# Four buffers instead of two for the second expert weights in an eight-core mixture-of-experts layer

## What is computed

```python
xn = layernorm(x)
att = (xn @ w_v.T + b_v) @ w_out.T + b_out          # softmax rows sum to 1
logits = xn @ router_w.T;  top2, idx = top_k(logits, 2);  w = softmax(top2)
h1 = gelu(xn @ w1[e].T + b1[e])                     # for each of 8 experts, 1024 -> 4096
y_e = h1 @ w2[e].T + b2[e]                          # 4096 -> 1024
out = x + att + sum over the two chosen e of w_e * y_e
```

## Time and profile before

| what | value |
|---|---|
| runs of the kernel before | 4571.72, 4616.52, 4870.86 us; median 4616.52 us |
| the profiled execution | 4570.31 us |
| its span on its slowest core (core 1) | 4568.8 us |
| TensorE matmul busy | 3863.4 us, 85% of the span |
| VectorE, ScalarE, GpSimd busy | 8%, 14%, 13% |
| weights moved by GpSimd's queue | 279.21 MB, 41.7% of the 16 DMA engines' time |

### The profile page before, as it was taken

How to read it: one execution, slowest core, us unless ns; L and a number is a source line. 1 busy time by engine, 2 the same in 40 slices (tenths; PEclk the granted TensorE clock), 3 DMA queues, 4 the chain that set the end, 5 groups by cost and what they waited for, 6 DMA issues and landing times.

```text
span 4568.8 us, 41331 instructions; the slowest of 8 cores (4540.7 to 4568.8 us)
## 1 busy us (share of the span) xinstructions
PE 3863.4 (85%) x17200; PEld 1662.0 (36%) x17200; DVE 372.7 (8%) x626; ACT 626.7 (14%) x610; POOL 575.3 (13%) x817
## 2 busy tenths in 40 slices
PE   2466889898989889898988989898988989898984
PEld 1222334343434334343433334343433434343431
DVE  4322010000000000100001010000000010000001
ACT  0122002030201112020201103020111202020200
POOL 1010111111111111111111011111111111111110
PEclk9687999999999999999999999999999999999997
DMA  4343344444444444444446244444444444453444
GB/s 76 51 60 50 43 64 70 64 70 60 74 60 73 63 66 68 60 72 60 75 60 142 45 62 72 60 76 56 72 64 67 67 62 72 60 81 53 72 61 101
DMA packets 251605, 307.02 MB, mean 67 GB/s; under 512 B 47591, under 2 KB 178663, under 8 KB 251424
## 3 DMA queue, kind: packets, MB, share of 16 engines
q0 software_dynamic: 244512, 279.21, 41.7%
q1 hardware_dynamic: 6912, 25.17, 1.7%
HBM read 574.89 MB, written 8.39 MB: 128 GB/s over the span
## 4 chain that ended last, share of the span: by engine, by line
PE 63%; DMA 25%; issue 5%; DVE 5%; ACT 1%; DVEq 0%; POOLq 0%; POOL 0%; SPq 0%; ACTq 0%
PE P L337 38%; PE P L416 22%; DMA wvw<-w2r 21%; DVE scr L430 3%; DMA wvw<-w1r 2%; DMA wvw<-wvf 1%; PE P L368 1%; PE P L187 1%; DMA x_rot<-x 1%; PE P L246 1%; ACT vg L349 1%; DVE xnF L252 0%; DMA b1c_sb<-b1c 0%; DVE scr L238 0%; DVEq L46 0%
## 5 line engine op out<-in xcount | busy, mean ns | idle before, releaser
L416 PE MATMUL P<-wvw,vg 128*128 128x512 bf16 x8192 | 1892.5, 385 | 394.5 <-DMA wvw<-w2r 335.1
L337 PE MATMUL P<-xnF,wvw 128*128 128x512 bf16 x8192 | 1787.1, 381 | 19.9 <-DMA wvw<-w1r 8.7
L416 PEld LDWEIGHTS P<-wvw,vg 128*128 128x128 bf16 x8192 | 778.7, 99 | 1505.9 <-issue 681.5
L337 PEld LDWEIGHTS P<-xnF,wvw 128*128 128x128 bf16 x8192 | 800.7, 98 | 1004.7 <-issue 57.9
L349 ACT ACTIVATE vg<-P,b1c_sb 128x1024 bf16<-128x1024 f32 x512 | 570.5, 1114 | 3224.7 <-PE P L337 3224.6
L393 POOL DMA_DIRECT2D wvw<-w2r x512 | 359.7, 703 | 2070.8 <-PE P L416 2001.8
L430 DVE SCALAR_TENSOR_TENSOR scr<-P,wmap_sb,scr 128x512 f32<-128x512 f32 x256 | 192.1, 750 | 3666.0 <-PE P L416 3642.0
L320 POOL DMA_DIRECT2D wvw<-w1r x256 | 180.0, 704 | 1585.3 <-PE P L337 1585.3
L187 PE MATMUL P<-xnF,wvw 128*128 128x512 bf16 x256 | 82.3, 485 | 44.8 <-DMA wvw<-wvf 44.8
L246 PE MATMUL P<-scr 128*128 128x128 f32 x128 | 28.5, 398 | 98.4 <-DVE scr L238 80.9
L187 PEld LDWEIGHTS P<-xnF,wvw 128*128 128x128 bf16 x256 | 28.3, 117 | 96.9 <-issue 84.1
(11 more groups left out here) (40 smaller groups left out, 176.6 us busy)
## 6 DMA issues: line engine op xcount, KB each, us to landing
wvw<-w1r POOLq DMA_DIRECT2D x256, 512.0 KB, 5.3
wvw<-w2r POOLq DMA_DIRECT2D x512, 256.0 KB, 4.1
x_rot<-x SPq DMA_DIRECT2D x32, 512.0 KB, 4.5
wvw<-wvf POOLq DMA_DIRECT2D x32, 256.0 KB, 5.0
out<-x_rot SPq DMA_DIRECT2D x16, 512.0 KB, 3.1
wo_sb<-wo POOLq DMA_DIRECT2D x8, 256.0 KB, 11.3
b1c_sb<-b1c POOLq DMA_DIRECT2D x1, 128.0 KB, 13.0
scr<-iden POOLq DMA_DIRECT2D x1, 64.0 KB, 5.8
```

Of the source, the lines that this page charges most:

```text
L337: pair=pair: t.matmul(pair[:, j * 512:(j + 1) * 512], w1sl[:, sl * 2048 + (f1c % 2) * 1024 + fc * 128: sl * 2048 + (f1c % 2) * 1024 + fc * ...
L416: t.matmul(W2B[tl], vg[:, f1c * 1024 + tl * 128: f1c * 1024 + (tl + 1) * 128], w2sl[:, sl * 1024 + (f1c % 2) * 512: sl * 1024 + (f1c % 2) ...
```

## The change

The w2 slots grow from two to four. The two new ones lie on the columns of `wvf_sl`. Each gets a semaphore of its own. The load of group g goes to slot g % 4 and so waits for the end of group g-4. The first load of each new slot has no w2 group before it; in its place it waits for the last matmul of the value projection (`tok_vpmm[(3, 7)]`), since that one still reads these columns. No instruction is added or taken away on TensorE, ScalarE or VectorE, and the number and size of the loads stay.

```diff
-    w2sl = wvw[:, 4096:6144]
+    w2sl = wvw[:, 4096:8192]
     wvf_sl = wvw[:, 6144:8192]
...
-            "dw2a", "dw2b", "dcst", "dwv", "dwo", "do0", "do1", "ddbg")
+            "dw2a", "dw2b", "dw2c", "dw2d", "dcst", "dwv", "dwo", "do0", "do1",
+            "ddbg")
...
-    DW2 = ("dw2a", "dw2b")
+    DW2 = ("dw2a", "dw2b", "dw2c", "dw2d")
...
-    nw2 = {0: 0, 1: 0}
+    nw2 = {0: 0, 1: 0, 2: 0, 3: 0}
...
             for g in range(NF1C // 2):
-                sl = g % 2
+                sl = g % 4
                 if tok_w2use.get(sl) is not None:
                     p.wait("gpsimd", "pe", tok_w2use[sl])
+                elif DO_B and sl >= 2:
+                    p.wait("gpsimd", "pe", tok_vpmm[(3, 7)])
                 nw2[sl] += 1
```

## The result

The changed kernel takes 4181.39 us (median of 10 runs, lowest 4178.03); the kernel before, run beside it, 4580.42 us (10 runs, lowest 4565.97). The ratio is 0.9141, with a 95% interval of 0.913 to 0.9152: 8.6% faster. Some executions of every kernel here are 1 to 18 per cent longer, with a lower granted clock on one die or both (of the ten of after 4238.86 and 4428.21 us, of the ten of before at least 4870.86 and 4995.08 us); ratios, and the times named for the experiments, leave these out.

The account below looks back on a forecast made before the run. W2 loads issued too late for two slots were taken to bound the kernel; W2 falling from 2287 to 1771 + 67 + 18 + 40 = 1896 us, taken as 390 us less, gave 4180 us, range 4125 to 4275 (80%).

Parts of the forecast that it names:

- part 1: W2 stages: loads issued earlier get three groups, 10.4 us, against 4.65 us needed; the usual load wait goes to nothing.
- the bound of 51 us: W2 loads: most that 15 late issues could cost if each gap met the worst landing, 3.4 us each time.
- Part 2: Change of sweep in W2: VectorE's freeing of banks keeps costing 4.2 us at each of 16 changes, 67 us.
- Part 3: W2 matmuls: 53 us of busy time come from a lower clock; 40 us after changes of sweep stay, 13 go.
- Part 4: Everything else: W2 starts keep 18 us; four w2 loads behind the last w1 load cost zero, at most 26 us.
- rival 3: End of h1 stages: the last w1 load pays; with both bounds 4257 us; no chance of its own given.
- The sum: W2 after: 1771 + 67 + 18 + 40 = 1896 us instead of 2287; 390 us taken off 4570.3 give 4180.
- The page on the load: Trainium skill's fit for a GpSimd load: 2.6 us per w2 load, so no wait to remove and 4570 us.
- Rival 1: W2 loads: DMA rate, not delay, limits; time near 4570 us (5%), or half-way 4280 to 4375 us (9%).
- Rival 2: Both matmul stages: denser load lowers the granted clock; gain used up at mean clock 0.90; chance 6%.

Follow-up runs that it names:

- two orders tried: Changed kernel with each sweep's last four chunks bank by bank: 4068.78 and 4071.10 us; that plus each W2 stage's first chunk with banks 4 to 7 first: 4051.71, 4051.11.
- the bank-wise order: Changed kernel with the matmuls of each sweep's last four chunks run bank by bank, four matmuls into each: 4068.78 and 4071.10 us.
- the extra loads: Changed kernel with w2 loads of the second half issued twice (experts 1 to 3) or every second one twice (experts 4 and 5): 4184.35 us.
- the wait two groups back: Changed kernel with four slots, but GpSimd waits for the end of group g-2 before load g: ratio to the kernel before 0.997, times from 4556.06 us.
- the held loads: Changed kernel with the third and fourth w2 load at each h1 stage's end held until h1 group 14 ends: first 4162.06, 4174.52, 4182.17 us; again 4165.75, 4165.90, 4181.32.

## Why the prediction was right

**What bounds the kernel, and part 1.** Both held. A load was issued and landed in 4.65 us where 3.46 us were to be had; with three groups of cover no wait for w2 loads is left, in any stage of any core. The landing is 4.1 us in the median as before, though the loads now come at a higher pace (73 GB/s in a W2 stage against 61). The late issues feared in part 1 are still there, 15 of them, one in each W2 stage but the first, each now a gap of 4.0 us:

```profile
POOL wvw L396 <- issue: 59.6, 15, 4.0
```

They cost nothing any more. Of the bound of 51 us for them nothing came true.

**Part 2.** The change of sweep is as long as before (6.88 us in the two shown). Predicted were 67 us for the sixteen and 18 for the starts, 85 in all; core 1 has 63.1 us of idle and 112 tails of 0.163 us, 18.3, which is 81.4 us. L419's wait for VectorE is 47.4 us, where I said about 50, from 42.0. The two orders tried put a price on both terms: with them, all of this waiting goes.

**Part 3.** Core 1's busy time is 1824.0 us; less 1771 and the tails it leaves 34.7 us at the lower clock. I had left 40 us in place, of 53, as a choice and not from a row that could decide it; it was the right one. That the pause at the change of sweep is what lowers the clock was my reading of two windows; the bank-wise order, which takes the pause away and the drop with it, shows it.

**Part 4** was the weakest step. I took zero for the w1 loads, with a bound of 26 us for the one load that has the four w2 loads right behind it. Against the kernel before, the mean wait for w1 loads went from 13.1 to 14.5 us only, and h1 on core 1 grew by 4.8 us. But the waits ahead of the last three groups of the h1 stages went from 0.9 to 5.7 us in the mean, and most of that (0.2 to 4.4) stands ahead of the last group but one, for a load that I had not looked at; ahead of the last group it is 0.2 to 0.9. The term should have been some 5 us. On core 0, which set the time, the wait for w1 loads is 20.9 us (15.1 before), just over the 20 that I had named as the sign of rival 3.

**The sum.** W2 was to go from 2287 to 1896 us and went to 1887.1 on core 1, the 9 us from parts 2 (81.4 for 85) and 3 (34.7 for 40). The spans: core 1's fell by 404.9 us (4568.8 to 4163.9), 395 of it in the two stages summed above and 9 before them (its first W2 matmul starts at 503.96 us, before at 513.09, though the change has no part in that stretch); core 0's fell by 373.5 (4551.6 to 4178.1), and the slowest core of each by 390.7; the mean over the eight cores fell by 387.9 (4553.2 to 4165.3). The cores differ by 25 us within one execution, the 390 were taken off one execution of the kernel before, whose median beside the changed kernel is 4580.42, and terms of 5 to 10 us came out wrong both ways. So that the forecast of 4180 met 4181.39 to about 1 us is luck; agreement to some 10 us isn't. I didn't think of another core becoming the slowest.

**The page on the load.** By the fit of the Trainium skill (DMA: Bandwidth & Descriptors, Anatomy of one DMA), taken with the 256 KB that land, there would have been nothing to win. The landing of 4.1 us, unchanged by the change, decides against it for this load, which is converted from float32 and runs beside seven other cores' loads.

**The rivals.** Rival 1 (rate) fell with the extra loads: twice the traffic, the same stages. Rival 2 (clock): the mean granted clock of the profiled executions is 0.963 before and 0.962 after on the median core, 1.00 in the h1 stages, and 0.99 over 3600 us in the kernel without pauses. By the rule of the Trainium skill (TensorE: Matmul & The Clock Gate, on the peak-current limiter) the whole change would have cost time, 817 us by the prediction's estimate. The traces agree with it in part only. In ten of the twelve profiled executions no core is granted 13/16 of the clock (0.81) for a single microsecond, with eight cores dense in matmuls for 3.6 ms. In the other two it is there: with the wait two groups back all eight cores are granted 0.81 for 818 to 887 us of the span, and in the first profile of the held loads cores 0 to 3 for 530 to 586 us. On core 6 of the former:

```profile
3710.00:3940.00 230.00, 221.28 (x835) 89.36 (x833) 8.85 (x12) 35.66 (x32) 26.00 (x37) 0.81 0.39 60
```

A whole h1 stage at that level takes 134.4 us instead of 110.5. That core had run its stages for three milliseconds before without it, so dense matmuls on all cores don't bring it on by themselves here; mean clocks as low (0.82) come with the kernel before as well, and what brings them on no run tells. Rival 3 came true in its small half, as said.

## What to carry to other kernels

Compare the time from a buffer's release to the landing of the next load with the time that the other buffers cover, in the timeline; if it is longer, one more buffer can win all of it, and the next one nothing (here two groups of cover did what three do). Before you count on a wait that goes, look what stands behind it at the borders of a stage: where banks are emptied one by one, order the last accumulations so that they finish at the pace of the engine that empties them. A pause of a few microseconds can have a second price in the clock that follows it, as it did here.

## What I had not expected of the hardware

The pause at a change of sweep, 7.4 us in which TensorE does 15 matmuls that need 3.2, is followed by some 7 us at a mean granted clock of 0.58 to 0.60; taking away 67 us of pauses gave another 35 us of matmul time. The DMA engines at a share of 0.96 (139 GB/s) let a 256 KB load land in 5.6 us instead of 4.0, so the share says little about waits as long as there is cover. And once in each W2 stage but the first GpSimd's stream stands for 4.0 us ahead of a load, at the same length in every stage of the changed kernel; what it does then the profile doesn't say, and it was not tried.
